# Graph attention with layer norm on one core: x W copied ahead of the one-hots, a counted staircase, three casts on ScalarE, two row blocks in halves

## The reference

```python
XW = jnp.matmul(X, W)
s_col = jnp.matmul(XW, a[0, :f])
s_row = jnp.matmul(XW, a[0, f:])
Z1 = jax.nn.leaky_relu(s_row[:, None] + s_col[None, :], negative_slope=0.01)
den = jnp.exp(Z1)
num = jnp.matmul(A, den)
att = jnp.where(num != 0, den / jnp.where(num != 0, num, 1.0), 0.0)
H = jnp.matmul(A, jnp.matmul(att, XW))
# result: layernorm(x + H)
```

## Time and profile before

| | |
|---|---|
| runs | 308.28, 309.94, 314.44 us (median 309.94) |
| the profiled execution | 308.92 us, of which the span of the profile is 307.2 us |
| mean granted TensorE clock | 0.926 of full |
| busy: PE, DVE, ACT, POOL | 268.5, 223.9, 191.2, 97.0 us |

### The profile page before, as it was taken

The page is one execution under the profiler, slowest core; times in us unless marked ns, Lnnn a source line. Parts: engine busy times, 40 slices in busy tenths (PEclk is TensorE's granted clock), DMA queues, the critical chain, the costliest instruction groups (busy, mean ns, idle before and its releaser), DMA issues.

```text
span 307.2 us, 5428 instructions
## 1 busy us (share of the span) xinstructions
PE 268.5 (87%) x1835; PEld 155.4 (51%) x1835; DVE 223.9 (73%) x363; ACT 191.2 (62%) x247; POOL 97.0 (32%) x95
## 2 busy tenths in 40 slices
PE   8793686987789999999998999999999626999994
PEld 3592435433344554455453445444444202999994
DVE  1778899989769999999957599899797710052274
ACT  2497058698799988769678887978688530000001
POOL 6501287998866475500000000075000063000000
PEclk9855569799799999999999999999999986999999
DMA  5000599618664355500000000001000063201111
GB/s 170 0 2 18 140 305 402 232 18 275 180 205 113 120 150 160 157 0 2 0 0 2 0 0 2 0 28 43 0 0 1 2 179 106 58 0 36 36 34 36
DMA packets 13942, 24.68 MB, mean 80 GB/s; under 512 B 1760, under 2 KB 8288, under 8 KB 13920
## 3 DMA queue, kind: packets, MB, share of 16 engines
q0 software_dynamic: 5632, 18.88, 19.1%
q1 hardware_dynamic: 8288, 5.50, 6.2%
HBM read 21.23 MB, written 3.15 MB: 79 GB/s over the span
## 4 chain that ended last, share of the span: by engine, by line
PE 47%; DVE 18%; ACT 8%; issue 7%; POOL 5%; DMA 4%; ACTq 1%; POOLq 0%; DVEq 0%; SPq 0%
PE ps L509 18%; PE ps L571 9%; PE ps L533 5%; PE ps L573 5%; DVE A L209 5%; PE ps L527 4%; DVE stage L1030 4%; POOL A L317 3%; DVE A L958 3%; DMA A<-adjT,perm 2%; POOL d_b L338 2%; PE ps L503 2%; PE ps L513 2%; ACT A L632 1%; ACT stage L713 1%
## 5 line engine op out<-in xcount | busy, mean ns | idle before, releaser
L509 PE MATMUL ps<-A,D 128*128 x372 | 87.5, 383 | 0.7 <-issue 0.3
L509 PEld LDWEIGHTS ps<-A,D 128*128 x372 | 36.4, 98 | 41.3 <-issue 9.9
L317 POOL DMA_INDIRECT A<-adjT,perm x31 | 45.4, 1464 | 26.7 <-DVE A L209 11.4
L338 POOL DMA_INDIRECT d_b<-crow,ranku x16 | 17.4, 1090 | 111.2 <-DVE crow L1048 72.8
L1030 DVE SCALAR_TENSOR_TENSOR stage<-ps,stage 128x1024 f32<-128x1024 f32 (+1 forms) x33 | 39.2, 1187 | 12.4 <-ACT stage L725 12.4
L713 ACT ACTIVATE stage<-ps 128x1024 f32<-128x1024 f32 (+1 forms) x33 | 32.9, 996 | 24.0 <-PE ps L513 23.9
L571 PE MATMUL ps<-D,A 128*128 128x256 f16 x256 | 42.4, 273 | 0.8 <-DMA D<-d_b 0.8
L573 PE MATMUL ps<-D,A 128*128 128x128 f16 x256 | 42.3, 219 | 0.0
L1034 DVE SCALAR_TENSOR_TENSOR stage<-rrow,cfloor,stage 128x1024 f32<-128x1024 f32 (+1 forms) x33 | 41.3, 1252 | 1.3
L209 DVE SCALAR_TENSOR_TENSOR A<-A,ecol 128x1024 f16<-128x1024 f32 x31 | 38.8, 1278 | 1.7 <-ACT A L632 1.1
L715 ACT ACTIVATE stage<-stage,epst 128x1024 f32<-128x1024 f32 (+1 forms) x33 | 37.0, 1123 | 1.1
(11 more groups left out here) (194 smaller groups left out, 391.7 us busy)
## 6 DMA issues: line engine op xcount, KB each, us to landing
tmp<-xT SPq DMA_DIRECT2D x4, 256.0 KB, 3.9
d_xw<-stage SPq DMA_DIRECT2D x1, 1024.0 KB, 5.1
D<-d_b SPq DMA_DIRECT2D x4, 256.0 KB, 3.6
out<-crow SPq DMA_DIRECT2D x3, 256.0 KB, 3.9
A<-adjT,perm POOLq DMA_INDIRECT x31, 5.1
xws<-d_xw,perm POOLq DMA_INDIRECT x16, 3.5
d_b<-crow,ranku POOLq DMA_INDIRECT x16, 2.3
out<-crow SPq DMA_DIRECT2D x1, 128.0 KB, 1.8
```

The source lines that it names most:

```text
L317: nc.gpsimd.indirect_dma_start(out=raw[n], out_offset=None, in_=rows, in_offset=bass.IndirectOffsetOnAxis(ap=perm[:, 0, h, b:b + 1], axis= ...
L338: nc.gpsimd.indirect_dma_start(out=d_b, out_offset=bass.IndirectOffsetOnAxis(ap=ranku[:, b:b + 1], axis=0), in_=Bn[:, b, :, :].rearrange(" ...
L509: nc.tensor.matmul(num[bank + c], D[:, d, bass.ds(slot, 1), :], A[:, h, bass.ds(k, 1), a, c * W:(c + 1) * W], start=False, stop=False, ski ...
```

## The change

It is made of these parts:

1. Rank: 5 flag buffers instead of 3 (`RING`; the two new ones lie in the tiles of A that the last two blocks of the second half take later), and ACT adds up 10 steps instead of 11 (`OWN`).
2. The first placing: DVE makes 9 of the 16 one-hots (`AHOT`); ACT makes 7, each with a Square and a Relu, after its copies of x W.
3. The counts of the staircase are made on PE: column totals of `hot`, their running sum, and comparisons of 16 or 15 partitions whose count a matmul with ones gives. Six wide or small DVE instructions of the staircase go (L901, L902, L920, L923, L925, L926) and `scales` has 3 instructions instead of 5; in their place come three small comparisons, of which one waits for PE (`upto`) ahead of the second `mark_places`. 2 of 10 warming matmuls there go too.
4. ACT reads the row of s_col in PSUM for the first two batches of logs and `weights(0)`; the copy to `crow` comes after `weights(0)`. Only 20 of 31 offsets are loaded there, the other 11 after item 0.
5. `OWN_CASTS` 1: block 14 of the first half has its high part made by ACT. The high parts of blocks 5, 8 and 11 of the second half are made by ACT too (`ACT_CASTS`); `CAST_AT` takes some blocks an item earlier.
6. Item 0 starts with a product that writes zeros, and its first product with the sums comes after the den products, so `w_lo` and `sums_sb` are waited for later.
7. The casts of x W to float16 are made at items 12 and 15 instead of 10 and 11.
8. `HALVED` 14: the last two J of h = 1 run as halves (30 full items and 4 halves). `half_bank` puts the first two halves into the banks of item 28, the others into those of item 29.

```diff
-OWN_CASTS = 2
-CAST_AT = ((1,), (2,), (3,), (4,), (5, 6), (7,), (8, 9), (10,), (11, 12), (13,), (14,), (15,))
+OWN_CASTS = 1
+CAST_AT = ((1,), (2,), (3,), (4, 5), (6,), (7, 8), (9,), (10, 11), (12,), (13,), (14,), (15,))
+ACT_CASTS = (5, 8, 11)
+RING = 5
-OWN = 11
+OWN = 10
+AHOT = 9
-HALVED = NB - 1
+HALVED = NB - 2
...
+        def half_bank(t):
+            i = t - FULL
+            return 2 * ((FULL + i // 2) % 2) + i % 2
...
             nc.tensor.matmul(bt[3][:, 0:NB * NB], ones16[:, :], hot[:, :], start=True, stop=True).then_inc(S["p_pre"], 1)
-            keep_warm(10, 2)
+            for j in range(NB):
+                mm = nc.tensor.matmul(num[3][0:NB, 0:1], hot3[:, :, j], onesb[:, :], start=(j == 0), stop=(j == NB - 1))
+            mm.then_inc(S["tot"], 1)
+            keep_warm(4, 2)
+            pe.wait_ge(S["tot_sb"], 1)
...
+            keep_warm(4, 2)
+            pe.wait_ge(S["cmp_lohi"], 1)
...
             place_sorted(1)
+            pe.wait_ge(S["cmp_slots"], 1)
+            nc.tensor.matmul(num[3][:, 64:64 + NS], ones16[0:NB - 1, :], slot_flags, start=True, stop=True).then_inc(S["p_slots"], 1)
...
-                if h == 0 and J % 4 == 0:
+                if h == 0 and J and J % 4 == 0:
                     pe.wait_ge(S["w_lo"], J // 4 + 1)
...
+            for b in range(AHOT, NB):
+                nc.scalar.activation(far[:, b - AHOT, :], ramp16[:, 0:P], ACT.Square, bias=place[:, 1, b:b + 1], scale=-1.0).then_inc(S["far"], 1)
+            for b in range(AHOT, NB):
+                act.wait_ge(S["far"], b - AHOT + 1)
+                nc.scalar.activation(lowhot[:, b, :], far[:, b - AHOT, :], ACT.Relu, bias=onesr[:, 0:1], scale=-1.0).then_inc(S["hots_act"], 1)
...
+                if 1 <= t <= len(CAST_AT) and CAST_AT[t - 1][-1] in ACT_CASTS:
+                    b = CAST_AT[t - 1][-1]
+                    act.wait_ge(S[f"g{b}"], 32)
+                    wait_lo(act, NB + b - 1)
+                    nc.scalar.activation(A[:, 1, b, 0, :], raw[NB + b], ACT.Copy, scale=ecol[:, b:b + 1]).then_inc(S["hi_late"], 1)
...
+            dve.wait_ge(S["upto"], 1)
+            V.tensor_scalar(upto_flags, cstt[0:NB, 4 + NB + NS:4 + 3 * NB + NS], num[1][0:NB, 64:65], None, ALU.is_ge).then_inc(S["cmp_lohi"], 1)
             mark_places(1, rankc[:, :])
```

More of the change, by code:

```diff
@@ L156, in graph_attention_layernorm @@
         onesr = xws[:, 1792:1792 + P]
-        flags = [D[:, :, :, :].rearrange("p a s j -> p (a s j)")[:, i * N:(i + 1) * N].bitcast(BF16) for i in range(3)]
+        flags = ([D[:, :, :, :].rearrange("p a s j -> p (a s j)")[:, i * N:(i + 1) * N].bitcast(BF16) for i in range(3)]
+                 + [A[:, 1, b, :, :].rearrange("p a i -> p (a i)").bitcast(BF16) for b in (NB - 2, NB - 1)])
         lowhot = flags[0].rearrange("p (b j) -> p b j", b=NB)
+        far = zlate[:, :].bitcast(BF16).rearrange("p (b j) -> p b j", j=P)
         hot = flags[2][:, 0:NB * NB]
@@ L192, in graph_attention_layernorm @@
         names = """b_late warm_sb p_rst rst_sb slot_hot p_slot in_w in_x0 in_x1 in_x2 in_x3 in_ws in_c p_wa wa_sb p_row p_col r_even r_odd rcol_sb ccol_sb p_xw xw_sb xw_out
-            const ramp flags flags_used flags_sum own vals_r vals_c pv where hots p_place perm_r perm_c rs_ready cs_ready thr hot p_pre top p_top rowtop cmax crow_t crow_sb
-            slots_ready mask_ready hi_done hi_dve lo_dve e_zero e_hi e_ready p_sums sums_hi sums_sb
+            const ramp flags flags_used flags_sum own vals_r vals_c pv where low_places far hots_act tot tot_sb upto cmp_lohi p_lohi cmp_slots p_slots hots p_place perm_r perm_c rs_ready cs_ready thr hot p_pre top p_top rowtop cmax crow_t crow_sb
+            slots_ready mask_ready hi_done hi_late hi_dve lo_dve e_zero e_hi e_ready p_sums sums_hi sums_sb
             m_ready e_exp v d_z d_exp d_lo bias_ready w_exp w_hi w_lo num_ready
@@ L412, in place_sorted @@
                 for b in range(NB):
-                    pe.wait_ge(S["hots"], i * NB + b + 1)
+                    if i == 0 and b >= AHOT:
+                        pe.wait_ge(S["hots_act"], b - AHOT + 1)
+                        pe.wait_ge(S["hots"], AHOT)
+                    else:
+                        pe.wait_ge(S["hots"], (AHOT if i else 0) + b + 1)
                     mm = nc.tensor.matmul(bt[1][:, 0:5 * NB], lowhot[:, b, :], moved[:, b, :, :].rearrange("p v h -> p (v h)"),
@@ L488, in add_num @@
                 h, J, c0, nc_ = ITEMS[t]
-                bank = (2 * (t % 2) if t < FULL else t % 4) - c0
+                bank = (2 * (t % 2) if t < FULL else half_bank(t)) - c0
                 cols = range(c0, c0 + nc_)
@@ L502, in add_num @@
                     o = h * H + c * W
+                    if t == 0:
+                        nc.tensor.matmul(num[bank + c], ident[0:1, 1:1 + P // 2].bitcast(F16), E[0:1, 0:4, :].rearrange("p b r -> p (b r)"),
+                                         start=True, stop=False, skip_group_check=True)
+                        continue
                     nc.tensor.matmul(num[bank + c][:, 0:HW], wgt[0:SUMROWS, J * P:(J + 1) * P], sums[0:SUMROWS, o:o + HW],
@@ L510, in add_num @@
                                              start=False, stop=False, skip_group_check=True)
+                if t == 0:
+                    pe.wait_ge(S["w_lo"], 1)
+                    pe.wait_ge(S["sums_sb"], 2)
+                    for c in cols:
+                        o = h * H + c * W
+                        nc.tensor.matmul(num[bank + c][:, 0:HW], wgt[0:SUMROWS, J * P:(J + 1) * P], sums[0:SUMROWS, o:o + HW],
+                                         start=False, stop=False, skip_group_check=True)
                 for c in cols:
@@ L596, in _ @@
                     act.wait_ge(S["flags_sum"], b - 1)
-                nc.scalar.activation(counted[b % 2][:, b * P:N], flags[b % 3][:, b * P:N], ACT.Copy, accum_out=above[:, b:b + 1]
+                nc.scalar.activation(counted[b % 2][:, b * P:N], flags[b % RING][:, b * P:N], ACT.Copy, accum_out=above[:, b:b + 1]
                                      ).then_inc(S["flags_sum"], 1)
@@ L675, in _ @@
             weights(0)
+            nc.scalar.copy(crow[:, :], crow_ps).then_inc(S["crow_sb"], 1)
+            act.wait_ge(S["crow_sb"], 1)
             def split_sums(c):
@@ L811, in mark_places @@
                                 vals[:, i, :, :].unsqueeze(3).to_broadcast([P, NB, 5, NB]), ALU.mult)
-                for b in range(NB):
+                for b in range(NB if i else AHOT):
                     V.tensor_scalar(lowhot[:, b, :], ramp16[:, 0:P], place[:, 1, b:b + 1], None, ALU.is_equal
@@ L1024, in _ @@
                     weights_low(WEIGHTS_AT[t - 1])
-                if 1 <= t <= len(CAST_AT):
+                if 1 <= t <= len(CAST_AT) and CAST_AT[t - 1][-1] not in ACT_CASTS:
                     residual(NB + CAST_AT[t - 1][-1])
@@ L1051, in _ @@
                     den_halves(LOWS_AT[t])
+                if 1 <= t <= len(CAST_AT) and CAST_AT[t - 1][-1] in ACT_CASTS:
+                    residual(NB + CAST_AT[t - 1][-1])
                 if t < len(CAST_AT):
```

100 lines of the change are left out of this document (55 added, 45 removed).

## The result

The changed kernel took 305.44 us (median of 6 runs, 304.80 to 312.84), the kernel before 309.37 on the same chip (6 runs, 308.28 to 314.44): ratio 0.987, interval 0.983 to 0.991. That is 4 us less and within 2%, as forecast; the time itself is 1.8 us under the forecast. On a second chip the changed kernel took 312.51 us (10 runs), 7 us longer, and the kernel before 313.64 (25 runs), 4 us longer: ratio 1.000, interval 0.995 to 1.004. So where it ran mattered as much as the change. Most of what follows is about what differs between the profiles; why the chips differ is not found.

What follows compares the result with a forecast made beforehand. PE's stream was taken as the bound: when it starts running, its holes, and the tail. Start -0.3, loop -1.5 and tail -0.4 sum to -2.2, from 309.4 to 307.2 us; range 302 to 310.5.

Steps and rivals of the forecast that it cites:

- -0.3: Start of the loop: ACT's square of item 0 at 83.15 us instead of 83.47.
- -1.5: Loop, item 2 to item 10: PE's 2.2 us of holes filled but for 0.7; from -2.2 to 0.
- -0.4: Tail: first late scatter goes out at 246.2 us instead of 246.61; from -1.5 to +0.5.
- The way to the first residual: Rank, placings and staircase: gathers start 1.9 us earlier, first residual (L209) at 47.75 us instead of 52.41.
- The placing's own part: First placing, one-hots split between DVE and ACT: 0.1 us earlier, from 0 to 0.5.
- So the slot values don't hold it: Before the run of residuals: PE turns the s_col row in 3.8 us, so the run begins at 50.25 instead of 54.91.
- That is where the stall goes: After the staircase: the residual run holds gather issues until 62.3 us; block 14 lands at 69.0, ACT idles from 62.3.
- Rival 2: No lock: gathers pass beside the residuals, square of item 0 at 78.4, 5.1 us earlier; sum -7.0, 302.4 us; chance 0.22.
- Rival 3: ACT becomes the loop's bound: 3.45 us of casts show in PE's stream, relief of 1.5 lost; 312.1 us; chance 0.10.
- the 246.2 for the first late scatter: Tail: chunk 2 complete at 242.4, DVE queued with items 31 and 32, first late scatter at 246.2 instead of 246.61.
- What would show it: Signs: first L209 about 47.8, POOL issue of some 11 us, item 0's square near 83, items 2 to 10 in 43.6.

Runs made afterwards that it cites:

- the kernel before with the hold: Kernel before, with POOL issuing no second-half gather until the residual of block 13 is done: 313.72 us, ratio 0.997, third chip.
- the kernel before with the same hold: Kernel before, with second-half gathers waiting for the residual of block 13, then three blocks ahead instead of six: 308.26 us, ratio 1.000, fourth chip.
- the one with three blocks ahead: Changed kernel with one block in halves and second-half gathers three blocks ahead instead of six, not waiting for block 13: 302.77 us, ratio 0.981, fourth chip.
- the hold alone: Changed kernel, with POOL issuing no second-half gather until the residual of block 13 is done, still six ahead: 313.34 us, ratio 0.996, third chip.

## Why the prediction was right, and where it was wrong

The forecast was 307.2 us with 302 to 310.5 around it and no difference over 2%; 305.44 came, a ratio of 0.987 to the runs beside it. The class and the range held. The sum inside held less well: -0.3, -1.5 and -0.4 made -2.2, and -4 came. The forecast's own account of the start did not happen, so that the time fell into its range is in part luck.

**The way to the first residual: right, a little too large.** I count from the first copy of the column. To the first gather it is 23.59 us (36.34 less 12.75) where it was 25.21, so 1.6 earlier and not 1.9. The placing's own part is as forecast, 2.45 us of products instead of 2.59. DVE waits 0.49 for `upto`, not 0.75. The second placing's last one-hot comes 1.0 earlier, and what stands behind it and the new comparison 0.8, where 1.1 was forecast; the first residual starts 37.66 after that copy instead of 41.95: 4.3 earlier, not 4.7. Every unmeasured cost here lay inside its bounds.

**"So the slot values don't hold it": wrong.** The prediction put this wait at nothing. PE was to turn the s_col row in 3.8 us. It took 4.60 in the profile after (48.84 to 53.44), with the clock at 1.2 GHz until 50.6, and 4.1 to 4.9 on the fourth chip. The copy waits 2.44 in the profile after, of which some 1.5 is behind the end of PE's product at 53.77, and 0.51 to 1.24 on the fourth chip. So the run of residuals begins 42.66 after the first copy instead of 44.45, 1.8 earlier and not 4.7, and on the fourth chip 3.0 to 3.7 earlier.

**"That is where the stall goes", the lock: wrong.** I took an issue of 11.76 us, seen once, for what always happens when residuals follow each other, and built the start of -0.3 on it. In twelve of the fourteen profiles of the case it doesn't happen (in one of them, the kernel before with the hold, no issue stands beside the run, and in another copies stand between the residuals). The run of the rows was ten residuals long, not twelve; the times worked out from it use ten. I had the mechanism (an issue that begins during a residual ends 0.82 after it) and the wrong condition; that of the phase could not be had from one profile, but that one could not is what the prediction should have said. Rival 2 was right on what POOL does. Its sum of the start can be checked on the fourth chip: 4.4 us earlier at the split of the sums (62.29 us from the first copy, against 66.72 in the kernel before with the same hold) where it said 3.7 (73.75 for 77.48). At item 0's square it is 68.02 against 71.47, 3.5 earlier and not 5.1, since ACT waits 1.09 there for PE's item 0, which stood behind the copy of the s_col row. Against the profile of before without a hold (73.01) it is 5.0.

**What the start was worth in the kernel as changed.** In the profiled execution, item 0's square comes at 75.13 from the first copy instead of 73.01: 2.1 later, for the starved stretch. With the start of the runs that have no such stretch (67.66 in the one with three blocks ahead) this execution would end 7.5 us sooner, at 303.6 us of span; the four short runs on that chip had 303.1 to 303.8. I conclude from this, without a profile of one of them, that they had no starved stretch, and that on the second chip nearly all had it. It is an argument and not shown: the start is taken from another chip, and this execution also began up to 2.4 us later than the others profiled, which the sum leaves in. If it is so, the errors in the forecast's sum were these: the start gained 3.5 us or more and not 0.3, and the tail lost 0.6 and gained nothing; with 1.4 from the loop that makes -4.3 beside the -3.9 measured. Where PE is starved, the start is 2 us later instead, and little is left of the gain.

**The loop: right.** -1.5 forecast, 1.37 seen in the first profile and 1.28 by giving the three casts back to DVE, with the order of before; the median went by 1.7. Rival 3, ACT as the bound, did not occur: in the window of the loop ACT is busy 59.07 of 68 us.

**The tail: the wrong sign.** -0.4 forecast, +0.6 to +0.7 seen, 0.6 given back by the run with one block in halves. The step that failed is the 246.2 for the first late scatter. DVE makes the copy of chunk 2 behind items 31 and 32, and in the profile after, item 32's first multiplication waits there for ACT:

```profile
245.82 0.69 DVE L1087 SCALAR_TENSOR_TENSOR stage<-ps,stage 128x512 f32<-128x512 f32 x1 [2.01 <-ACT stage L783]
246.55 0.75 DVE L1091 SCALAR_TENSOR_TENSOR stage<-rrow,cfloor,stage 128x512 f32<-128x512 f32 x1
247.22 0.68 DVE L1063 COPY rrow<-ps 128x512 f32<-128x512 f32 x1
```

I had named that queue and priced it too low.

**What would show it.** The times that follow are shifted so that the first copy stands where it stood before, at 10.46. First residual at 47.8: 48.1 in both profiles of the changed kernel. A long issue that ends 0.8 after the run: absent. Square of item 0 near 83: 85.6 and 85.9. Item 2 to item 10 in 43.6: 43.8. Late slot values were named as what would make the prediction wrong, with a slow clock as the cause. They came, and part of the turn ran at 1.2 GHz in each of these profiles; but so it did on the fourth chip, where the wait is 0 to 1.24 us. The clock accounts for about that much, and not for the 3.3 to 4.1.

## What to carry to other kernels

A change that lets transfers run beside PE has to be followed into PE: here the gathers passed freely, as one would wish, and beside the last of them PE took one matmul each 2.1 us. Spreading such a burst (here three blocks ahead and not six) took 8 us off the hold alone, and is worth trying before what comes ahead of it is shortened. And a wait that stands in one profile of a kernel, however long, is one draw: whether it belongs to the program or to a phase is only seen in a second profile, best from another chip.

## What the runs showed of the hardware

- PE can stand without a wait for a semaphore towards the end of a long row of gathers by POOL: weight loads up to 2.1 us apart, in stretches of about 1 us (before, second and third chip) to 12 us (with the hold alone), which end within about 2 us of the last issue or transfer. In all profiles where it occurs the gathers had run for 13 us or more. But they also ran from 68 to 90 us in the kernel before on the first chip and from 35 to 66 us on the fourth (three ahead, no hold), without it; what decides stays open. What PE lacks then is not in the trace. I looked at the two queues that carry instructions: 22 packets in the whole span, and none lies in the gaps of 69.5 to 75.2 (one at 59, one at 64.7, the next at 95). The Trainium skill, "Runtime: NRT & Kernel Launch", section "Instruction fetch mechanics", calls crossing from one block of instructions to the next mostly hidden; a gap that stays at one time while the instructions under it change speaks for something else than such a crossing. All of this is from recorded executions, so I can't tell whether the recording has a share in it.
- After such a stretch PE's granted clock is at its lower level, 1.2 GHz, for 3.4 to 6.9 us, and the warming matmuls meant to keep it up take 1.91 us for four instead of 1.03. Without them it stays there longer, 10.2 us, and item 0 comes earlier all the same.
- A software gather's issue and a run of DVE instructions with two SBUF inputs can settle in either of two ways: after the first, all issues pass at 0.94 us with the run stretched by 3%, or one issue is held for the whole run, 11.76 and 11.74 us.
- The kernel before took 309.4 and 308.1 us on two chips and 313.6 and 314.6 on two others. On the slower ones the copy of the slot values came 3.3 to 4.1 us late in every profile, that of the kernel before included.
